# Both groups of probability transposes placed behind the fourth chunk of scores in a Perceiver block

## The reference

```python
x = x + xattn(layernorm(x), ctx)        # x: 256 x 2048, ctx: 25088 x 2048, float32

def xattn(query, key):                  # the values are the keys
    a = einsum('bqd,bkd->bqk', query, key)
    e = softmax(a, axis=-1)
    return einsum('bqk,bkd->bqd', e, key)
...
x = x + attn(layernorm(x), Wq, bq, Wk, bk, Wv, bv)
x = x + ffn(layernorm(x), W_base, b_base, W_gate, A, B)
```

## Time and profile before

| | |
|---|---|
| median of 3 runs | 2508.55 us (2503.86, 2508.55, 2513.61) |
| the profiled execution | 2506.24 us |
| its span, first to last instruction | 2504.5 us |
| mean granted TensorE clock | 0.994 |
| PE busy | 2453.2 us, 98% |
| DVE busy | 1948.7 us, 78% |
| ACT busy | 1093.8 us, 44% |
| POOL busy | 1420.5 us, 57% |

### The profile page before, as it was taken

The page is one execution under the profiler, slowest core; times in us unless marked ns, Lnnn a source line. Parts: engine busy times, 40 slices in busy tenths (PEclk is TensorE's granted clock), DMA queues, the critical chain, the costliest instruction groups (busy, mean ns, idle before and its releaser), DMA issues.

```text
span 2504.5 us, 36094 instructions
## 1 busy us (share of the span) xinstructions
PE 2453.2 (98%) x11446; PEld 2009.8 (80%) x11446; DVE 1948.7 (78%) x2702; ACT 1093.8 (44%) x1576; POOL 1420.5 (57%) x1056
## 2 busy tenths in 40 slices
PE   6999999999999999999999999999999999999899
PEld 4788888888888888888888888888888888877677
DVE  7878888888888888888788887888878878674356
ACT  4444444444444444444444444444444444333443
POOL 4466666666666555565566565565555655652441
PEclk9999999999999999999999999999999999999899
DMA  9887878888788988889888988888888898778633
GB/s 239 212 229 203 229 210 220 224 206 229 206 229 217 224 206 219 222 211 218 212 219 204 230 212 204 219 217 219 211 219 216 205 222 217 199 169 155 153 122 101
DMA packets 421112, 518.22 MB, mean 207 GB/s; under 512 B 54407, under 2 KB 296071, under 8 KB 418441
## 3 DMA queue, kind: packets, MB, share of 16 engines
q1 hardware_dynamic: 411080, 475.66, 77.9%
q0 software_dynamic: 9984, 41.95, 5.0%
HBM read 488.71 MB, written 28.84 MB: 207 GB/s over the span
## 4 chain that ended last, share of the span: by engine, by line
PE 92%; DVE 3%; DMA 2%; SPq 1%; ACT 1%; issue 0%; POOL 0%; ACTq 0%; POOLq 0%
PE ps L1435 30%; PE ps L1437 30%; PE ps L1436 29%; PE ps L1444 2%; DMA tr<-wt_dram 2%; DVE ch_lo L1061 1%; SPq L429 1%; DMA raw<-in_ctx_dram 1%; SPq L559 0%; DVE tr L1057 0%; PE ps L1656 0%; DVE nat_lo L1201 0%; PE ps L1729 0%; PE ps L1602 0%; PE ps L1463 0%
## 5 line engine op out<-in xcount | busy, mean ns | idle before, releaser
L608 POOL TENSOR_TENSOR nat_lo<-raw,nat_hi 128x512 fp32r<-128x512 f32 x784 | 1170.9, 1523 | 874.0 <-ACT nat_hi L767 841.2
L1061 DVE TENSOR_TENSOR ch_lo<-tr,ch_hi 128x512 fp32r<-128x512 f32 x784 | 849.0, 1083 | 369.2 <-ACT ch_hi L756 369.2
L756 ACT CAST ch_hi<-tr 128x512 fp32r<-128x512 f32 x784 | 477.2, 621 | 807.6 <-PE ps L1437 799.4
L1435 PE MATMUL ps<-ch_hi,xt_hi 128*128 128x512 f32 x1696 | 680.1, 401 | 19.0 <-DVE ch_lo L1061 7.9
L1437 PE MATMUL ps<-ch_hi,xt_lo 128*128 128x512 f32 x1696 | 665.0, 392 | 0.0
L1436 PE MATMUL ps<-ch_lo,xt_hi 128*128 128x512 f32 x1696 | 664.1, 392 | 0.0
L1435 PE MATMUL ps<-nat_hi,pt_hi 128*128 128x512 f32 x1568 | 611.7, 390 | 2.1 <-DVE pt_lo L1010 2.1
L1437 PE MATMUL ps<-nat_hi,pt_lo 128*128 128x512 f32 x1568 | 610.3, 389 | 0.0
L1436 PE MATMUL ps<-nat_lo,pt_hi 128*128 128x512 f32 x1568 | 610.1, 389 | 0.0
L1057 DVE STREAM_TRANSPOSE tr<-quart 128x512 f32<-128x512 f32 x784 | 547.1, 698 | 0.0
L767 ACT CAST nat_hi<-raw 128x2048 fp32r<-128x2048 f32 x196 | 374.5, 1911 | 207.3 <-PE ps L1437 194.5
(11 more groups left out here) (199 smaller groups left out, 1312.7 us busy)
## 6 DMA issues: line engine op xcount, KB each, us to landing
quart<-in_ctx_dram SPq DMA_DIRECT2D x392, 512.0 KB, 8.3
raw<-in_ctx_dram SPq DMA_DIRECT2D x196, 1024.0 KB, 8.3
wq_in<-in_L_attn_Wq_dram POOLq DMA_DIRECT2D x16, 1024.0 KB, 6.3
win<-in_L_ffn_W_base_dram SPq DMA_DIRECT2D x64, 256.0 KB, 6.8
tr<-wt_dram POOLq DMA_DIRECT2D x64, 256.0 KB, 3.2
wt_dram<-stage SPq DMA_DIRECT2D x32, 256.0 KB, 5.6
wt_dram<-stage_b SPq DMA_DIRECT2D x32, 256.0 KB, 10.3
wq_dram<-wq_out POOLq DMA_DIRECT2D x16, 256.0 KB, 2.3
```

Source lines behind the costliest of these rows:

```text
L608: last = pool.tensor_tensor(nat_lo[:, j, t], raw[:, j % 2, t], nat_hi[:, j, t].bitcast(F32), ALU.subtract)
L756: act.copy(ch_hi[:, c % RING_CH, :], tr[:, c % RING_TR, :]).then_inc(chunk_hi, 1)
L1061: dve.tensor_tensor(ch_lo[:, c % RING_CH, :], tr[:, c % RING_TR, :], ch_hi[:, c % RING_CH, :].bitcast(F32), ALU.subtract).then_inc(chunk_s ...
L1435: pe.matmul(out_, a_hi, b_hi, start=start, stop=False)
```

## The change

In TensorE's order, and only there, group 0 leaves its place behind chunk 2. Both groups now stand behind chunk 3, and where the turn has a late piece 7, behind that:

```diff
@@ -1512,8 +1512,9 @@
                     chunk_scores(turn, c)
                     if c in LATE_AFTER and lagging:
                         late_piece(turn, LATE_AFTER[c])
-                    if c in (2, 3) and not turn.first:
-                        probs_group(turn, c - 2)
+                    if c == 3 and not turn.first:
+                        for q in range(TT):
+                            probs_group(turn, q)
                     if c in PIECE_AFTER and not turn.first:
                         weighted_piece(turn, PIECE_AFTER[c])
```

## The result

The changed kernel takes 2558.5 us (median of 4 runs, 2556.3 to 2559.7) against 2508.0 for the kernel before (4 runs). The ratio is 1.0203, with a 95% interval of 1.0183 to 1.0223: slower by 50.5 us, where 43 were forecast and the likeliest time was 2551. The profiled execution took 2559.69 us with a span of 2557.9 us, 53.4 more than before; the mean granted clock is 0.994 in both.

The account below looks back on a forecast made before the run. TensorE's queue was taken as the bound; 31 turns at 0.76 + 0.18 us and 16 at 0.76 + 0.10 give 43 us, 2549 profiled, so median 2551; own range 2540 to 2562, overall 2533 to 2565.

Parts of the forecast that it names:

- What bounds it: Key-block turns: only TensorE's own queue counts, 98% busy, so any pause added there is paid in full.
- When group 0 is drained: ScalarE and VectorE behind the first four transposes: `pt_lo` 0 starts at 5.34 instead of 3.37, `pt_lo` 1 ends at 8.47.
- W0: `weighted_piece` 0, the twelve TensorE matmuls that wait until VectorE has written both `pt_lo` halves.
- When W0 starts: TensorE, from the third chunk's end: 8.52 against 7.76 us, 0.05 after `pt_lo` 1, with 0.79 us idle each turn.
- The restart: W0's matmuls after the pause: 2.90 instead of 2.72 us, 0.18 more; only 0.10 new in sixteen turns.
- The sum: Over 47 turns: 31 x (0.76 + 0.18) and 16 x (0.76 + 0.10), 43 us slower.
- The cover holds: Rival: VectorE's two subtractions end by 7.5, so W0 has no pause; 1 to 3 us saved, 2506; chance 0.07.
- GpSimd in the way: Rival: GpSimd's subtraction slows VectorE's `lo_chunk` 7 by 1.1 us each turn, 52 us in all, 2603; chance 0.03.
- The clock: Rival: each new TensorE pause brings 3.3 us at half clock, losing 1.65 us; 78 us more, 2629; chance 0.04.

Follow-up runs that it names:

- the dose: The changed kernel with only VectorE's late addition 7 moved from ahead of `pt_lo` 1 to behind it: 2526.6 us, ratio 1.0078.
- both orders: The changed kernel with ScalarE and VectorE also taking both groups together, TensorE's order untouched: 2503.8 us, ratio 0.9985.
- the half move: The kernel before, with group 0 moved past chunk 3 only and kept ahead of late piece 7: 2510.0 us, ratio 1.0010.
- the reordered waits: The changed kernel with the wait for the low halves (`lo_drained`) put last of the three ahead of weighted piece 0: 2547.0 us, ratio 1.0161.

## Why the prediction came out as it did

**What bounds it: right.** TensorE paused in none of the turns with late pieces before, so the new pause was paid in full.

**When group 0 is drained: right to 0.01 us.** Forecast from group 0: copy at 0.64, `pt_lo` 0 at 1.26, `pt_lo` 1 done at 4.39, group 1 at 0.44. Measured: 0.64, 1.26, 4.40, 0.44. VectorE's five instructions kept the length they had in the earlier trace rows, as taken. In the turn of the earlier trace rows, which shows only the last of the five, the trace has 0.65, 0.67, 0.69, 0.70 and 0.68 for them.

**When W0 starts: the term that was too small.** The forecast was 8.52 us from the end of the third chunk, measured 4.08 + 4.62 = 8.70. The prediction took 0.05 for the step from `pt_lo` to TensorE, from the one wait at the end of the key loop. That row stands outside the loops, with constant wait values; in the loops two register steps follow the wait, and the step is 0.22. 44 turns by 0.17 is 7.5 us. The 0.31 of the earlier trace rows, which the prediction read only as a restart cost, was the trace's own sign of it: W0 started slowly there with `pt_lo` 0.24 us early.

**The restart: too large.** W0's twelve matmuls take 2.855 us on average, 0.13 more than 2.72, where 0.18 was taken. In the turns that had a slow W0 before (14, not 16) they took 2.83, so only 0.02 is new there instead of 0.10. Together that is 2.6 us less.

**The sum.** 43 + 7.5 - 2.6 = 47.9. Counted from the end of chunk 2 in the second turn to the end of the loop, the profiled changed kernel is 48.4 us longer; the 0.5 left is 0.01 a turn. The second turn, for which 0 and at most 2 us was said, takes 46.63 us to the end of the third turn's chunk 2 instead of 46.60: 0 was right. Of the profile's 53.4, another 1.2 lie ahead of the first instruction that was moved, and 3.7 behind the loop, where profiles of these kernels differ by as much (302.9 to 308.9). These 5 us can't be put down to the change; that the medians differ by 50.5 and not by 48.4 may be the same spread.

**The rivals.** *The cover holds* fell: W0 waits in each turn. The threshold that it named, 2.1 us from the start of the first subtraction to the end of the second, lies between what the experiments tried: 2.5 in the dose, where W0 still waits, and 1.29 with both orders, where it doesn't. *GpSimd in the way*: it did not meet `lo_chunk` 7, which took 0.68; it began at 1028.72, behind it and during `pt_lo` 1:

```profile
1028.72 6.01 POOL L608 TENSOR_TENSOR nat_lo<-raw,nat_hi 128x512 fp32r<-128x512 f32 x4 [5.94 <-ACT nat_hi L767]
```

*The clock* stayed at 1.00 in the pause and behind it, and from 70 us to the end of the loop. Columns as in the earlier trace rows:

```profile
1028.00:1029.20 1.20, 0.41 (x2) 0.00 (x0) 1.20 (x3) 1.20 (x3) 0.47 (x1) 1.00 1.12 207
1029.30:1032.00 2.70, 2.70 (x12) 2.24 (x13) 2.67 (x4) 0.38 (x1) 2.70 (x3) 1.00 1.13 288
```

A pause of 1 us in each turn did not bring the oscillation of which the Trainium skill warns (TensorE: Matmul & The Clock Gate, section HAM oscillation — how this bites in real kernels); no run here has a longer one in each turn.

## What to carry to other kernels

Before a producer's step is moved on one engine, follow it through the fixed orders of the engines behind it: the price is not the step's own delay but the unrelated instructions queued between its product and the next one that the consumer needs. Work out two slacks in the old profile. One is the time between the product being ready and the engine behind it coming to it: it made the half move free. The other is the consumer's margin (here 1.26 us) against the new lateness of what it waits for (1.97): what is over is paid once a turn, and the dose gave it back at the same rate. Where the consumer has several waits whose values are worked out in registers, put the one that comes last in time last in the program; with constant values that order was the slower one here. Take hand-over times from rows inside the loop that is meant, not from one outside it.

## What the runs showed of the hardware

With wait values worked out in registers, the two further waits behind the one that came last delayed TensorE: from VectorE's end to the matmul's start it was 0.22 us with both behind, and 0.05 with none. With constant values it was 0.06 with both behind and 0.15 with none. The profile's list hides this: it put 40 us of TensorE's waiting down to `pt_lo`, and for the weight loads named VectorE's additions into `acc`, which the reordered waits and the dose showed to be innocent:

```profile
PEld ps L1435 <- DVE acc L1108: 55.1, 44, 1.3
```

Behind a pause of 0.2 to 1.0 us the next twelve matmuls took longer as well, 2.82 to 2.89 us instead of 2.72; most of it lies between the first and the second (0.33 instead of 0.23). A small VectorE operation on 128x2 elements took 1.10 us beside a running GpSimd subtraction, instead of 0.15:

```profile
1028.93 1.10 DVE L1089 TENSOR_TENSOR denom_s<-denom,alpha 128x2 f32<-128x2 f32 x1
```

This happened in nearly every turn of the changed kernel and makes its VectorE busier, without a cost in time. The operation has two SBUF operands, as `lo_chunk` has. The Trainium skill (SBUF — State Buffer, section SBUF: two separate sides) describes such an exclusive lock between the two engines, and the number agrees with it; `pt_lo` 1, which reads PSUM, took its usual 0.68 while GpSimd began.
